# A wait in the middle of a chunk's eight gathers, in a graph convolution on one core

## The reference

```
xs = x[src]
deg_w = max(seg(edge_weights), 1); deg_c = max(seg(1), 1)
norm  = edge_weights / sqrt(deg_w[src] * deg_w[dst])
gcn   = seg(norm * xs) @ Wgcn + bgcn
sage  = x @ Wsage_s + seg(xs) / deg_c @ Wsage_n + bsage
agg_w = seg(edge_weights * xs)
gin   = ((1 + gin_eps) * x + agg_w) @ Wgin + bgin
gconv = x @ Wgc1 + agg_w @ Wgc2 + bgc
eop   = seg(edge_weights * relu(xs + edge_attr)) @ Wedge + bedge
out   = layernorm(x + weights . [gcn, sage, gin, gconv, eop])
```

## Time and profile before

| | |
|---|---|
| median of three runs | 2213.24 us |
| profiled execution | 2228.75 us |
| its span, first to last instruction | 2226.9 us |
| TensorE matmuls busy | 1556.4 us |
| VectorE busy | 928.6 us |
| ScalarE busy | 826.9 us |
| GpSimd busy | 1355.2 us |

### The profile page before, as it was taken

How to read it: one execution, slowest core, us unless ns; L and a number is a source line. 1 busy time by engine, 2 the same in 40 slices (tenths; PEclk the granted TensorE clock), 3 DMA queues, 4 the chain that set the end, 5 groups by cost and what they waited for, 6 DMA issues and landing times.

```text
span 2226.9 us, 22565 instructions
## 1 busy us (share of the span) xinstructions
PE 1556.4 (70%) x6037; PEld 1007.5 (45%) x6037; DVE 928.6 (42%) x2539; ACT 826.9 (37%) x1201; POOL 1355.2 (61%) x1426
## 2 busy tenths in 40 slices
PE   1004367566888777877878778777887888877876
PEld 1003367553554544544445445444444445544546
DVE  5684256543433332433433433243333334423346
ACT  1676233243433433424244234233333324423323
POOL 7665366556666656656666666566666656665660
PEclk9999967688989888978889888888888888888988
DMA  5111234331222222222222222222222222222223
GB/s 98 23 24 51 70 100 112 95 80 42 51 64 45 55 54 46 57 46 44 54 57 53 47 57 43 47 58 50 48 66 43 48 51 57 47 53 44 59 55 77
DMA packets 83186, 126.12 MB, mean 57 GB/s; under 512 B 29494, under 2 KB 31269, under 8 KB 82821
## 3 DMA queue, kind: packets, MB, share of 16 engines
q0 software_dynamic: 45056, 48.85, 13.6%
q1 hardware_dynamic: 36371, 74.90, 11.0%
q10 hardware_dynamic: 1650, 1.04, 0.2%
HBM read 121.29 MB, written 3.40 MB: 56 GB/s over the span
## 4 chain that ended last, share of the span: by engine, by line
PE 43%; issue 18%; another core or an unknown queue 17%; DVE 10%; ACT 4%; POOL 3%; DVEq 2%; DMA 1%; SPq 0%; POOLq 0%; ACTq 0%
PE psum L1280 27%; PE psum L1261 13%; ACT ring L604 4%; POOL ring L559 3%; DVE ring L1076 2%; DVE sums L1065 2%; DVE early L988 1%; PE psum L1312 1%; PE psum L1228 1%; DVE attr L953 1%; DVE early L992 1%; DMA ring<-node_table,idx 1%; PE psum L1341 1%; PE psum L1342 1%
## 5 line engine op out<-in xcount | busy, mean ns | idle before, releaser
L559 POOL DMA_INDIRECT ring<-node_table,idx x1280 | 1228.4, 960 | 758.2 <-issue 389.4
L1280 PE MATMUL psum<-table_sb,early_x 128*128 128x455 f32 x2240 | 988.1, 586 | 115.6 <-issue 110.1
L1280 PEld LDWEIGHTS psum<-table_sb,early_x 128*128 128x128 f32 x2240 | 446.0, 205 | 573.4 <-issue 566.7
L1261 PE MATMUL psum<-ring 128*128 128x120 f32 x2560 | 405.3, 313 | 246.5 <-issue 127.5
L1261 PEld LDWEIGHTS psum<-ring 128*128 128x128 f32 x2560 | 375.5, 224 | 310.2 <-issue 164.9
L988 DVE TENSOR_TENSOR early<-psum,digit_hot 128x455 f32<-128x455 f32 x160 | 100.6, 631 | 989.5 <-remote 599.3
L688 ACT ACTIVATE early_x<-early,minus_ids 128x256 f32<-128x256 f16 x560 | 370.4, 744 | 138.7 <-remote 103.4
L655 ACT ACTIVATE ring<-attr 128x512 f32<-128x512 f32 x160 | 100.2, 626 | 483.4 <-DVE attr L953 383.8
L679 ACT ACTIVATE early<-early 128x256 f32<-128x256 f32 x40 | 16.7, 416 | 518.2 <-DVE early L1009 385.1
L1065 DVE TENSOR_TENSOR sums<-sums,psum 64x40 f32 (+1 forms) x648 | 127.5, 197 | 97.4 <-remote 53.6
L526 POOL DMA_INDIRECT early_x<-in_x,early_idx x128 | 122.0, 953 | 61.4 <-issue 40.3
(11 more groups left out here) (158 smaller groups left out, 644.8 us busy)
## 6 DMA issues: line engine op xcount, KB each, us to landing
attr<-in_edge_attr SPq DMA_DIRECT2D x79, 512.0 KB
ring<-node_table,idx POOLq DMA_INDIRECT x1280
early<-in_edge_attr SPq DMA_DIRECT2D x36, 256.0 KB
src_all<-in_src SPq DMA_DIRECT2D x16, 512.0 KB
early<-key_rows SPq DMA_DIRECT2D x10, 512.0 KB
early_x<-degree_rows SPq DMA_DIRECT2D x2, 1568.0 KB
early_x<-in_x,early_idx POOLq DMA_INDIRECT x128
node_table<-table_sb SPq DMA_DIRECT2D x1, 1666.0 KB, 6.0
```

What stands on the lines that cost most here:

```text
L559: nc.gpsimd.indirect_dma_start(out=feat[:, u, j, D:BLOCK], out_offset=None, in_=table, in_offset=bass.IndirectOffsetOnAxis(ap=idx[:, u, j: ...
L1261: last = nc.tensor.matmul(to[:, 0:3 * WINDOW], features[:, j, 0:2 * D], hots[:, j].rearrange("p k n -> p (k n)"), start=(j == 0), stop=(j ...
L1280: last = nc.tensor.matmul(pick_ps[k % 2].rearrange("p (b c) -> p b c", b=SPLIT), node_hot[:, k, a], table_sb[:, a * SPLIT:(a + 1) * SPLIT, ...
```

## The change

GpSimd issues the first four gathers of a late chunk as before. Ahead of the fifth (`j == HALF`, HALF = 4) it waits until these four have landed: `gathered[u]` has 128 for every earlier chunk of that place and 64 for these four. Then it counts `gathers_begun` up once more and issues the other four. Nothing else is changed; the waits of VectorE and ScalarE are as they were.

```diff
                         pool.wait_ge(chunk_product, it + 1)
                         pool.sem_inc(gathers_begun, 1)
                         for j in range(TILES):
+                            if j == HALF:
+                                pool.wait_ge(gathered[u], (v * LATE_STEPS + i) * (16 * TILES) + 16 * HALF)
+                                pool.sem_inc(gathers_begun, 1)
                             nc.gpsimd.indirect_dma_start(
```

## The result

| | before | after |
|---|---|---|
| median of the runs | 2212.56 us | 2276.26 us (2271.19 to 2280.92) |
| profiled execution | 2228.75 us | 2275.57 us |
| its span | 2226.9 us | 2273.8 us |

After takes 1.0288 times as long as before, 95% interval 1.0261 to 1.0315: slower by 64 us, where 8 were predicted. The time is above the range, whose upper end was 2261.

What follows compares the result with a forecast made beforehand. The prediction took TensorE and the engines feeding it to bound the loop, with gathers ahead. Main loop 3 us plus loop end 5 us made 8 us: 2236.8 profiled, 2221.2 us median; the forecast's own range 2217 to 2238, overall 2207 to 2261.

Steps and rivals of the forecast that it cites:

- What bounds the kernel: Late loop, 700 to 2100 us: runs at the pace of TensorE and the two engines handing it operands; gathers run ahead.
- 2.1 us a chunk to spare: GpSimd's true waiting, 700 to 2100 us: 241 us over 115 chunks, of the 12.15 us a chunk takes.
- the stall: GpSimd's added idle ahead of each fifth gather: 1.9 us a chunk, bounds 1.65 and 2.4; 304 us over 160 chunks.
- 2.15 landing: Time from the fourth gather's start until its packets landed, read from a gather with the queue to itself: 2.15 us.
- 0.75 wake: From GpSimd's semaphore instruction after a real wait to the next gather's start: 0.75 us.
- 0.25 lag: From a gather's last packet to its semaphore: 0.25 us taken, bounds 0 and 0.9.
- this row, 2.9 us: Landing of a gather issued at 1056.16 beside a stream of edge attributes: 2.9 us, giving the stall's upper bound 2.4.
- the first rival: Main loop: GpSimd becomes the bound if the stall is 2.4 against 2.1 spare; 46 us plus 5, 2264 us; chance 0.17.
- The sum: Whole kernel: 3 us in the main loop plus 5 at its end, 8 us; 2236.8 profiled, 2221.2 median.
- The lead of the ring: Main loop: four-place ring, GpSimd three chunks ahead, covers lateness of a few us; loss 3 us, bounds 0 and 25.
- The end of the loop: Last chunk: its fourth gather's landing is delayed by the degree rows' broadcasts, so the final VectorE read slips 5 us.
- The rival "faster": Loop: fewer gather packets let other loads through, and TensorE gets full clock more often; 2204 us; chance 0.11.

## Why the prediction was wrong

- **What bounds the kernel** was read half right. TensorE was on the path, and GpSimd had 2.1 us a chunk to spare. Why it had them was not asked: the pace of 12.15 us goes with completions that came 5 us late while GpSimd streamed gathers. The prediction set the two side by side as independent, and they are not. In every kernel that waits for a landing in each chunk (mean idle 2.3 us and more), VectorE's 599 us of "remote" waits at the picks are gone. The completions come on time (after, median 0.01 us late) or at the latest in the pause (wait ahead of the seventh gather, 144 of 160), and GpSimd alone is left to set the pace.
- **The term that failed is the stall.** I put 2.15 landing - 1.25 + 0.75 wake + 0.25 lag = 1.9. Measured, without the one chunk told of below: landing 2.61, wake 0.75 in every case, from the last packet to GpSimd's semaphore instruction a mean of 0.47 (median 0.36): 2.61 - 1.25 + 0.75 + 0.47 = 2.58. The wake and the undisturbed landing were right: a median of 2.13 to 2.14 for the first, second and fifth to eighth gathers of a chunk. The landing that is waited for was not undisturbed: the 2.15 taken for it is the step that failed, for it measured 2.61. Once the ring has no lead (VectorE begins a chunk a median of 0.4 us behind its last landing, before 18.8), VectorE, ScalarE and the attribute load run in step with GpSimd, and the load falls on the third and fourth gathers of every second chunk: the mean idle there is 3.28 us, in the others 2.49. The prediction had this row, 2.9 us, and used it for the upper bound of the stall alone. Its own signs for the first rival all came: the fifth gathers' idle is a mean of 2.9 us and not 2.2, VectorE and ScalarE wait for gathers all through the loop, and the gathers hold 49% of the chain.
- **The sum.** GpSimd's own chunk is 10.04 + 2.58 = 12.62 us against before's 12.21 between the marks of the table: 0.41 x 155 = 64 us. That these are also the 64 us between the medians is chance: the 12.21 is of an execution of before 16 us above its median, and its repeat of 2197.29 us took 12.01. Halfway between the two, an estimate, the loop loses 89 us, the start and the last chunk give back 28 and the rest costs 2, which makes 63. The rival "GpSimd becomes the bound", from a stall of 2.1 on, is what happened. Its 2264 us came from a stall of 2.4, 0.3 over the spare, and left out the start. By the Trainium skill, DMA: Bandwidth & Descriptors, section "Anatomy of one DMA — SWDGE (gpsimd) path", about 2.0 us of fixed cost gave an estimated stall of 2.5. That is near the 2.58, but for another reason: the undisturbed landing comes 1.2 us behind the end of the gather's instruction, or 1.6 with the lag to the semaphore, not 2.0, and what is missing is the attribute load. The section's about 100 ns for the semaphore's update count from the write's receipt, which no row shows; the trace has 0.36 from the last packet.
- **The lead of the ring** was no help. A ring four chunks deep covers a lateness that ends. This one was there in each chunk, and the loop used up the lead and then ran at GpSimd's pace.
- **The end of the loop.** The prediction had the last chunk's landing caught by the degree rows' broadcasts, for 5 us. In after the broadcasts were issued at 2187.86 us, three chunks ahead of the end, and caught another landing. GpSimd, VectorE and GpSimd again at the end of after:

```profile
2202.30 0.94 POOL L562 DMA_INDIRECT ring<-node_table,idx  x1 [12.42 <-DMA ring<-node_table,idx]
...
2208.54 0.22 DVE L953 TENSOR_TENSOR psum<-e_w,ring 128x8 f32<-128x8 f32 x1 [15.19 <-DMA ring<-node_table,idx]
...
2226.28 0.94 POOL L562 DMA_INDIRECT ring<-node_table,idx  x1 [2.33 <-DMA ring<-node_table,idx]
```

  This took 12.42 - 2.6 = 9.8 us, inside the 73.8 of the table, and the last chunk was free of it: 8.3 us less there. The mechanism was right, its place was three chunks off, and the two nearly cancel: +1.5.
- **The start of the loop** was not looked at. The prediction's stretches began at 700 us, or asked only who waits for gathers. The 20 us that the waits bring there hid that the loop cost 74. With the predicted stall of 1.9 GpSimd's own chunk would be 11.94 us, under before's 12.01 to 12.21, and by this estimate the change would have won time, as the wait ahead of the seventh gather did with 2.04.
- **The rival "faster".** My reason against it, that no engine waits for an attribute load in the steady part, holds. The gain at the start came from a cause that the rival did not name. Its other half, a clock granted more often, gave nothing: 0.867 before and 0.872 after, and TensorE's matmuls are busy 9.6 us a chunk in both (700 to 1700 us).

What stays open: by what path unbroken gathers delay TensorE's completions, and in the run with the wait ahead of the loop its instructions too; why they do so in one condition and not in the other; and whether a pause of over 2 us without a landing would do as well. The DMA records don't tell the conditions apart: over 300 to 1700 us a packet of the gather queue took a mean of 109 ns in before and 103 in its copy with the wait ahead of the loop under the prompt condition.

## What to carry to other kernels

Read each "spare" of an engine as what another's lateness leaves it, and ask what makes that lateness; a wait released by "remote" long behind the end of the matmuls' records is not a wait for their work. Where a stall comes within a few tenths of the spare, compute the stalled engine's own pace (here 8 x 0.95 + 8 x 0.30 + stall) against the loop's and take the landing beside the traffic that the new rhythm brings, since a deep ring doesn't help against a stall in each round. A wait that hurts in a loop can help in its first rounds, so try it there alone: the wait in the first four chunks gained 1.1% both times under the late condition, and a pause in the same place cost 0.4 to 0.5% under the prompt one.

## What the hardware showed that I had not expected

- The same kernel took 2206 to 2213 us in four groups of runs and 1830 in two. Under the late condition TensorE's completions came a median of 5 us after the records' ends while gathers followed one another every 1.25 us; under the prompt one, in the profiles of its copy with the wait ahead of the loop, 0.01 us after them with the same gathers. The granted clock was 0.867 in the profile of before, and 0.939 to 0.940 in those of its copy with the wait ahead of the loop under the prompt condition.
- The change's price depends on that: 1.03 where completions are late. The prompt condition was not run with it; with its stall of 2.6 an estimate is 1830 + 155 x 2.6 = 2233 us, ratio 1.22, beside the 1.184 measured for a stall of 2.1.
- A pause of 1.3 us ahead of the fifth gather let 7 of 160 completions through, a wait of 2.4 us ahead of the seventh 144.
- From GpSimd's semaphore instruction, which ends its wait, to the start of the next gather it takes 0.75 us, in 160 of 160 cases of after within 0.01 us.
